# A GNN–LSTM–GNN kernel: one LSTM chain is set four steps behind the other, and two batches of each end's layers go between turns of a single chain

## The chip, the cores and the metric

The kernel runs on one core of a Trainium2 chip. The metric is device microseconds of one execution; less is better. All data is float32. TensorE multiplies in its float32r form; a float32 operand is split into a high part and a remainder, and a product is three matmuls (high × high, high × low, low × high).

## The reference

`x` is [16, 512, 128] (batches, tokens, features), `adj` is [512, 512]. What is computed is:

```
h  = relu(layernorm(x))
h  = relu(adj @ (h @ Wg0 + bg0));  h = relu(adj @ (h @ Wg1 + bg1))      # per batch
for p in 1..4:                      # windows of p tokens, the last token of each is replaced
    wins = h[:, :nw*p].reshape(16*nw, p, 128)                           # nw = 512 // p
    h[:, p-1::p] = last hidden state of an LSTM with weights p over wins  # p steps
x  = x + h
g  = relu(layernorm(x))
A_hat = D^-1/2 (adj + I) D^-1/2
t  = relu(batchnorm((A_hat @ g) @ W1.T + b1))      # 256 features, statistics over all 16*512 rows
x  = x + batchnorm(t @ W2.T + b2)                  # 128 features
```

## The kernel before, in words

It is written engine by engine; each engine runs a fixed list of instructions, and semaphores tie the lists together. The order of the lists is set by tables of numbers at the head of the file.

**LSTM turns.** Features lie on the partitions, tokens along the free axis. The 16 batches go in four rounds of four; a round has two chains, each of two batches (`CHAINS`, `SUBS`). A chain makes 11 turns a round (`STEPS`, L40): two for p=1 (one per batch, 512 windows), then the 2, 3 and 4 steps of p=2, 3, 4 for both batches together (512, 340 and 256 windows). A turn (`lstm_turn`: TensorE L1087, ScalarE L580, VectorE L814) is: gate products into PSUM banks (three gates on the first step of a window, four after), sigmoid/tanh on ScalarE (L598), cell update on VectorE (L836 to L844), tanh of the cell on ScalarE (L608), hidden state on VectorE (L849/L851 between the steps of a window, L870 at its end). On steps after the first the input tokens need their own split: the high part on ScalarE (L606), the low part on GpSimd (`later_class`, L352 to L356). A p=1 turn ends with four VectorE operations: odd tokens into `cell` (L857), their high part (L859) and low part (L669), and the even tokens into `h32` (L864).

**Slots.** `ORDER` (L41) sets the 22 turns of a round in a row: the p=1 turns of chain 0 and 1 first, then step for step the one chain after the other. A turn is a slot; 88 slots in all. The slot loops (TensorE L1114, VectorE L875, ScalarE L611, GpSimd L358) put other batches' work behind the turns, from two tables:

- `PRE_POS` (L99): layer norm of `x` ("stats" on VectorE, then `layer_norm` on GpSimd, L328 to L340, then "norm", the hi/lo split, L550 and L664) and four product units `AGG0`, `LIN0`, `LIN1`, `AGG1` of the first GNN, for the batches of the next round. `EARLY = 4`: those of batches 0 to 3 lie in a prologue (`PROLOGUE`, L264), as does part of batch 4's.
- `POST_POS` (L101): for the batches of the round before, "turn" (transpose back and residual, L1047 and L759), "stats" and "norm" of the second layer norm, "agg" (A_hat product, L1055), "hid0", "hid1" (the two halves of the W1 product, L1062, with a PSUM eviction L573 and statistics L770). Those of the last four batches (12 to 15) lie in a tail (L1143).

In round 0 the slots also hold the degree sums of `adj` (`deg_steps`, L1066) and four chunks of A_hat (`HAT_CHUNK`, L774 to L788 on VectorE). SyncE issues the loads, stores and spills in one list (from L403).

**Final stage.** After the statistics of all batches comes batch norm 1. Scale and shift of its 32 halves of 512 tokens (L389) are on GpSimd (30) and VectorE (2, `DVE_HALVES`); ScalarE takes relu and the high part (L648), VectorE the low part (L667), TensorE the W2 product, ScalarE its eviction (L641), VectorE its statistics (L944). Then come batch norm 2 (L658, L398), transposes and the residual.

Of the kernel before, what the change touches and what calls it, by code (L numbers as in the profile page):

```python
# [21 lines left out]
ALU = mybir.AluOpType  # L22
# [68 lines left out]
DVE_HALVES = (0, 1)  # L91
# [3 lines left out]
EARLY = PER_ROUND  # L95
# [7 lines left out]
IN_PROLOGUE = [(kind, EARLY + b) for kind, spots in PRE_POS.items() for b in range(PER_ROUND) if spots[b] < 0]  # L103
PRE_AFTER = [[(kind, n) for kind, spots in PRE_POS.items() for n in range(EARLY, BATCHES)
              if len(ORDER) * (n // PER_ROUND - 1) + spots[n % PER_ROUND] == slot] for slot in range(N_SLOTS)]
POST_AFTER = [[(kind, n) for kind, spots in POST_POS.items() for n in range(LATE)
               if len(ORDER) * (n // PER_ROUND + 1) + spots[n % PER_ROUND] == slot] for slot in range(N_SLOTS)]


DEG_SUM, DEG_TOKENS, DEG_POW, DINV_DIAG, DINV_ROWS = 3, 3, 4, 5, 7  # L110
HAT_CHUNK = (8, 11, 14, 17)
# [13 lines left out]
def build(nc, x, adj, Wg0, bg0, Wg1, bg1, Wih, Whh, bih, bhh, W1, b1, g1, be1, W2, b2, g2, be2, out):  # L125
# [7 lines left out]
    with whole:  # L133
# [13 lines left out]
        minus_half, minus_one, eps = (sb(n, [P, CHUNKS]) for n in ("minus_half", "minus_one", "eps"))  # L147
# [28 lines left out]
        ln_pre = [sb(f"ln_pre{i}", [P, 3, CHUNKS]) for i in range(2)]  # L176
        ln_post = [sb(f"ln_post{i}", [P, 3, CHUNKS]) for i in range(2)]
# [39 lines left out]
        def f32(ap):  # L217
# [36 lines left out]
        t_dve, t_pool, hid_hi, hid_lo, out_mm, z2_ready, z2_stats = (  # L254
            sem(n) for n in ("t_dve", "t_pool", "hid_hi", "hid_lo", "out_mm", "z2_ready", "z2_stats"))
# [10 lines left out]
        for _pair in range(2):  # L266
            for _k in range(4):
                PROLOGUE += [(_k, 2 * _pair), (_k, 2 * _pair + 1)]
                if _k in (AGG0, LIN1) and _pair == 0:
                    PROLOGUE += [("stats" if _k == AGG0 else "norm", n) for n in (2, 3)]  # L270
                if _k in (AGG0, LIN1) and _pair == 1:
                    PROLOGUE += [(kind, n) for kind, n in IN_PROLOGUE if kind == ("stats" if _k == AGG0 else "norm")]
                if 6 + 4 * _pair + _k < len(BANKS):
                    PROLOGUE.append(("bank", 6 + 4 * _pair + _k))

        def pre_number(n, k):

            return 8 * (n // 2) + 2 * k + n % 2 if n < EARLY else 4 * n + k

# [34 lines left out]
        def _(pool):  # L314
# [6 lines left out]
            for tile, value in ((minus_half, -0.5), (minus_one, -1.0), (eps, EPS)):  # L321
# [6 lines left out]
            def layer_norm(n, y, src, mv, ln, stats, ready):  # L328
# [4 lines left out]
                nc.gpsimd.tensor_tensor(ln[:, 2, :], mv[:, :, 0], minus_one[:, :], ALU.mult)  # L333
# [23 lines left out]

            for slot in range(N_SLOTS):  # L358
                r, chain, p, step, sub, nb = TURNS[slot]
                if p >= 3 and step + 1 < p:  # L360
                    later_class(r, chain, p, step + 1)
# [11 lines left out]
            for n in range(LATE, BATCHES):  # L373
# [10 lines left out]
            for k, b in enumerate(END_ORDER):  # L384
                if b < SPILLED:
                    pool.wait_ge(z_in[b], 16)
                for half in ((1,) if k in DVE_HALVES else (0, 1)):
                    zz = z_end(b)[:, half * T:(half + 1) * T]
                    last = nc.gpsimd.tensor_scalar(zz, zz, bn1[:, 4, half:half + 1], bn1[:, 5, half:half + 1],  # L389
                                                   ALU.mult, ALU.add)  # L390
                last.then_inc(t_pool, 1)
# [11 lines left out]
        def _(sp):  # L403
# [42 lines left out]
            for r in range(ROUNDS):  # L446
                m, n = PER_ROUND * (r + 1), PER_ROUND * (r - 1)
                if r == 0:
                    load_x_pre(m)
                    load_x_pre(m + 1)  # L450
# [51 lines left out]
        def _(act):  # L502
# [77 lines left out]
            def lstm_turn(g):  # L580
# [4 lines left out]
                for j, gt in enumerate(gates_of(step)):  # L585
                    if prev is not None and TURNS[prev][2] == 1:

                        if gt == G_GATE:
                            act.wait_ge(h_done, prev + 1)
                            act.wait_ge(even_done, FIRST_BEFORE[prev + 1])  # L590
# [7 lines left out]
                    nc.scalar.activation(gate[:, tile_of(g), gt, 0:size], gate_ps[k % GATE_BANKS][:, 0:size],  # L598
# [607 lines left out]
```

## Time and profile before

| | |
|---|---|
| time, median of 3 runs | 613.42 us (611.78 to 615.2) |
| the profiled execution: its own time / its span | 614.24 us / 612.4 us |
| TensorE matmul busy | 526.4 us (86%), 2769 matmuls |
| VectorE busy | 434.4 us (71%) |
| ScalarE busy | 349.7 us (57%) |
| GpSimd busy | 208.2 us (34%) |
| mean granted TensorE clock | 0.947 |
| first gate matmul starts | 71.31 us |
| last hidden state written | 518.05 us |
| batch norm 1 starts | 548.71 us |

The span runs from the first to the last instruction. Stages by time: up to 71 us prologue; 71 to 518 us the 88 turns (rounds 0 to 3 of 113, 117, 117 and 99 us from last tanh to last tanh, the first from the stage's start); to 549 us the tail's layers; then the final stage. A busy figure of TensorE includes the drain of each matmul, which overlaps the next.

### The profile page before, as it was taken

The numbers are of one execution on the slowest core, as the hardware profiler recorded it, in microseconds if no ns is written. First come the engines' busy times: TensorE is split into PE (matmuls) and PEld (weight loads), VectorE is DVE, ScalarE is ACT, GpSimd is POOL, SyncE is SP. The second block draws the span as 40 slices with busy tenths as digits, with TensorE's granted clock in tenths as the row PEclk, the third lists the DMA queues.
The fourth block names the chain that finished last, engine by engine and source line by source line (L and its number), as shares of the span: only waits on it lengthen the run. The fifth ranks groups of instructions, "written<-read, shape, count | busy, mean of one in ns | idle before, by whom it ended". The sixth has DMA issues, their size and how long they took to land.

```text
span 612.4 us, 8136 instructions
## 1 busy us (share of the span) xinstructions
PE 526.4 (86%) x2769; PEld 450.7 (74%) x2769; DVE 434.4 (71%) x985; ACT 349.7 (57%) x660; POOL 208.2 (34%) x316
## 2 busy tenths in 40 slices
PE   4579899698999899999989999998699988766646
PEld 3467768597987688988977798997487988545436
DVE  3364476877886888778588887866867876557766
ACT  2523565555556567666665665756647765245654
POOL 2241003311340266247005560600143240809951
PEclk9769999989899999999999999999989989796997
DMA  6200002000001110202011101004510000500007
GB/s 215 78 4 33 2 0 87 18 18 1 18 1 36 51 52 34 71 1 70 25 62 51 36 35 52 18 35 153 226 34 1 18 18 14 194 0 0 0 0 276
DMA packets 17837, 31.21 MB, mean 51 GB/s; under 512 B 1498, under 2 KB 6020, under 8 KB 17796
## 3 DMA queue, kind: packets, MB, share of 16 engines
q1 hardware_dynamic: 17092, 30.30, 14.5%
q8 instruction: 22, 0.36, 0.3%
q10 hardware_dynamic: 704, 0.39, 0.2%
q14 instruction: 19, 0.16, 0.1%
HBM read 19.16 MB, written 11.53 MB: 50 GB/s over the span
## 4 chain that ended last, share of the span: by engine, by line
PE 47%; issue 23%; DVE 11%; POOL 11%; ACT 4%; POOLq 2%; DVEq 0%; ACTq 0%
PE gate_ps L972 10%; PE gate_ps L974 9%; PE gate_ps L973 9%; POOL z_back L389 5%; PE pre_ps L973 3%; PE pre_ps L974 3%; PE pre_ps L972 3%; POOL x_pre L338 3%; PE post_ps L972 2%; PE post_ps L974 2%; PE post_ps L973 2%; POOLq L336 2%; ACT gate L608 1%; POOL z_ring L389 1%; ACT gate L598 1%
## 5 line engine op out<-in xcount | busy, mean ns | idle before, releaser
L598 ACT ACTIVATE gate<-gate_ps,gate_bias 128x256 f32<-128x256 f32 (+2 forms) x312 | 166.6, 565 | 55.6 <-PE gate_ps L974 53.1
L972 PE MATMUL gate_ps<-by_class_hi,wih_hi 128*128 128x256 f32 (+2 forms) x264 | 86.8, 329 | 14.1 <-POOL by_class_lo L356 7.2
L608 ACT ACTIVATE gate<-cell 128x512 f32<-128x512 f32 (+2 forms) x88 | 45.3, 515 | 77.7 <-DVE cell L844 41.8
L974 PE MATMUL gate_ps<-by_class_lo,wih_hi 128*128 128x256 f32 (+2 forms) x264 | 85.2, 323 | 0.0
L973 PE MATMUL gate_ps<-by_class_hi,wih_lo 128*128 128x256 f32 (+2 forms) x264 | 85.1, 322 | 0.0
L972 PEld LDWEIGHTS gate_ps<-by_class_hi,wih_hi 128*128 128x128 f32 x264 | 51.4, 195 | 21.3 <-POOL by_class_lo L356 8.0
L972 PE MATMUL gate_ps<-hstep_hi,whh_hi 128*128 128x256 f32 (+2 forms) x192 | 61.5, 320 | 0.0
L973 PE MATMUL gate_ps<-hstep_hi,whh_lo 128*128 128x256 f32 (+2 forms) x192 | 61.5, 320 | 0.0
L974 PE MATMUL gate_ps<-hstep_lo,whh_hi 128*128 128x256 f32 (+2 forms) x192 | 61.4, 320 | 0.0
L332 POOL TENSOR_TENSOR ln_pre<-mv_pre,eps 128x4 f32<-128x4 f32 x16 | 5.0, 314 | 159.2 <-DVE mv_pre L713 159.2
L356 POOL TENSOR_TENSOR by_class_lo<-h,by_class_hi 128x256 fp32r<-128x256 f32 (+1 forms) x40 | 35.3, 890 | 61.2 <-ACT by_class_hi L606 61.2
L973 PEld LDWEIGHTS gate_ps<-by_class_hi,wih_lo 128*128 128x128 f32 x264 | 51.4, 195 | 3.8
L974 PEld LDWEIGHTS gate_ps<-by_class_lo,wih_hi 128*128 128x128 f32 x264 | 51.2, 194 | 2.3
L332 POOL TENSOR_TENSOR ln_post<-mv_post,eps 128x4 f32<-128x4 f32 x16 | 6.1, 381 | 136.7 <-DVE mv_post L713 136.7
L849 DVE TENSOR_TENSOR gate<-gate 128x256 f32<-128x256 f32 (+2 forms) x48 | 26.9, 560 | 26.4 <-ACT gate L608 26.4
L973 PEld LDWEIGHTS gate_ps<-hstep_hi,whh_lo 128*128 128x128 f32 x192 | 37.8, 197 | 1.3
L974 PEld LDWEIGHTS gate_ps<-hstep_lo,whh_hi 128*128 128x128 f32 x192 | 37.7, 197 | 1.3
L972 PEld LDWEIGHTS gate_ps<-hstep_hi,whh_hi 128*128 128x128 f32 x192 | 37.7, 196 | 1.3
L338 POOL TENSOR_SCALAR x_pre<-x_pre,ln_pre 128x128 f32<-128x128 f32 x64 | 35.7, 569 | 2.8 <-issue 2.8
L338 POOL TENSOR_SCALAR y_post<-x,ln_post 128x128 f32<-128x128 f32 x56 | 34.8, 633 | 2.5 <-issue 2.5
L838 DVE TENSOR_TENSOR gate<-gate 128x256 f32<-128x256 f32 (+2 forms) x48 | 24.3, 507 | 15.8 <-ACT gate L598 15.8
L389 POOL TENSOR_SCALAR z_back<-z_back,bn 128x512 f32<-128x512 f32 x24 | 29.7, 1253 | 0.0
(249 smaller groups left out, 1406.7 us busy)
## 6 DMA issues: line engine op xcount, KB each, us to landing
x_pre<-in_x SPq DMA_DIRECT2D x16, 256.0 KB, 2.6
x<-in_x SPq DMA_DIRECT2D x16, 256.0 KB, 2.8
z_spill<-z_ring SPq DMA_DIRECT2D x8, 512.0 KB, 2.7
z_back<-z_spill SPq DMA_DIRECT2D x8, 512.0 KB, 7.4
x_spill<-x SPq DMA_DIRECT2D x12, 256.0 KB, 2.0
x_back<-x_spill SPq DMA_DIRECT2D x1, 3072.0 KB, 11.1
out<-x_back SPq DMA_DIRECT2D x12, 256.0 KB, 2.2
x<-in_adj SPq DMA_DIRECT2D x1, 1024.0 KB, 5.5
```

The costliest lines, as they stand in the source:

```text
L332: nc.gpsimd.tensor_tensor(ln[:, 0, :], mv[:, :, 1], eps[:, :], ALU.add)
L336: nc.gpsimd.drain()
L338: last = nc.gpsimd.tensor_scalar(y[:, c * P:(c + 1) * P], src[:, c * P:(c + 1) * P], ln[:, 2, c:c + 1], ln[:, 1, c:c + 1], ALU.add, ALU.mult)
L356: nc.gpsimd.tensor_tensor(lo, states, f32(hi), ALU.subtract).then_inc(later_lo, 1)
L389: last = nc.gpsimd.tensor_scalar(zz, zz, bn1[:, 4, half:half + 1], bn1[:, 5, half:half + 1], ALU.mult, ALU.add)
L598: nc.scalar.activation(gate[:, tile_of(g), gt, 0:size], gate_ps[k % GATE_BANKS][:, 0:size], ACT.Tanh if gt == G_GATE else ACT.Sigmoid, bia ...
L608: nc.scalar.activation(gate[:, tile_of(g), G_GATE, 0:size], cell[:, tile_of(g), 0:size], ACT.Tanh)\
L838: nc.vector.tensor_tensor(i_, i_, g_, ALU.mult).then_inc(ig_done, 1)
L849: nc.vector.tensor_tensor(i_, o_, g_, ALU.mult).then_inc(h_done, 1)
L972: nc.tensor.matmul(ps, w[0], m[0], start=start, stop=False)
L973: nc.tensor.matmul(ps, w[1], m[0], start=False, stop=False)
L974: return nc.tensor.matmul(ps, w[0], m[1], start=False, stop=stop)
```

## The change

- **Slots.** A round still has 22 turns, but chain 0 has the even slots and chain 1 the odd ones, and chain 1 runs `LAG = 4` steps behind. There are 97 slots. Slots 1, 3, 5 and 7 have no turn and slots 0, 2, 4, 6 and 8 one of chain 0; slots 89 to 95 have turns of chain 1 alone, 88 to 96 even ones none.
- **Input layers.** `EARLY` goes from 4 to 2: in the prologue stay, of batch 2, "stats", "norm", `AGG0` and `LIN0`; the rest of batch 2 goes to slots 1 and 3, batch 3 to slots 3 to 9.
- **Output layers.** The tail has batches 14 and 15 alone (`TAIL`); those of 12 and 13 lie in slots 88 to 96. All positions of `PRE_POS` and `POST_POS` are new, as are those of the degree sums and A_hat chunks. The list of SyncE follows.
- **Even tokens** of a p=1 turn: off VectorE (L864), onto ScalarE as a copy out of `cell` (L639 of the new file). In the new file VectorE's next first cell update waits for it.
- **Layer norm on GpSimd** loses one of its small operations: the mean is no longer multiplied by −1 (L333), it is subtracted straight from `mv`.
- **Batch norm 1 halves**: GpSimd 30 → 25, VectorE 2 → 1, ScalarE 0 → 6.

```diff
-ORDER = ([(chain, s) for chain in range(CHAINS) for s in range(SUBS)]
-         + [(chain, s) for s in range(SUBS, len(STEPS)) for chain in range(CHAINS)])
-N_SLOTS = ROUNDS * len(ORDER)
+LAG = 4
+ROUND = CHAINS * len(STEPS)
+N_SLOTS = ROUND * ROUNDS + CHAINS * LAG + 1
+def step_in(slot):
+    chain = slot % CHAINS
+    r, s = divmod(slot // CHAINS - LAG * chain, len(STEPS))
+    return (r, chain, s) if 0 <= r < ROUNDS else None
...
-DVE_HALVES = (0, 1)
+DVE_HALVES = ((0, 0),)
+ACT_HALVES = ((0, 1), (3, 1), (5, 1), (8, 1), (11, 1), (14, 1))
...
-EARLY = PER_ROUND
-PRE_POS = {"stats": (-5, 4, 7, 13), "norm": (-2, 6, 10, 16),
-           AGG0: (0, 8, 13, 18), LIN0: (1, 10, 14, 19), LIN1: (2, 11, 15, 20), AGG1: (4, 12, 17, 21)}
-POST_POS = {"turn": (0, 1, 2, 3), "agg": (6, 9, 14, 19), "hid0": (7, 10, 16, 20), "hid1": (8, 11, 17, 21),
-            "norm": (5, 7, 12, 17), "stats": (3, 5, 9, 15)}
+EARLY = SUBS
+TAIL = BATCHES - SUBS
+PRE_POS = {"stats": (6, 11, 15, 25), "norm": (8, 13, 18, 26),
+           AGG0: (10, 16, 20, 27), LIN0: (11, 17, 21, 28), LIN1: (13, 18, 23, 29), AGG1: (15, 19, 25, 31)}
+POST_POS = {"turn": (0, 1, 9, 10), "agg": (3, 6, 13, 16), "hid0": (4, 7, 14, 17), "hid1": (5, 8, 15, 18),
+            "norm": (2, 5, 12, 15), "stats": (0, 2, 9, 12)}
...
-HAT_CHUNK = (8, 11, 14, 17)
+HAT_CHUNK = (10, 13, 16, 19)
...
                 nc.gpsimd.tensor_tensor(ln[:, 0, :], mv[:, :, 1], eps[:, :], ALU.add)
-                nc.gpsimd.tensor_tensor(ln[:, 2, :], mv[:, :, 0], minus_one[:, :], ALU.mult)
...
+            def even_tokens(g):
+                r, chain, p, step, sub, nb = TURNS[g]
+                act.wait_ge(h_done, g + 1)
+                if r > 0:
+                    act.wait_ge(turn_mm, batch_of(r - 1, chain, sub) + 1)
+                nc.scalar.activation(h32[:, chain, 0::2, sub], cell[:, chain, 0:T // 2], ACT.Copy)\
+                    .then_inc(even_done, 1)
...
+            for slot, g in enumerate(TURN_AT):
+                if g is not None:
+                    lstm_turn(g)
                 for splits in (True, False):
+                    if not splits and g is not None and TURNS[g][2] == 1:
+                        even_tokens(g)
...
+            def hid_t(k, half):
...
+                nc.scalar.activation(zz, zz, ACT.Identity, bias=bn1[:, 5, half:half + 1],
+                                     scale=bn1[:, 4, half:half + 1]).then_inc(t_act, 1)
...
+                    if PREV[g] is not None and TURNS[PREV[g]][2] == 1:
+                        before = TURNS[PREV[g]]
+                        dve.wait_ge(even_done, FIRST_BEFORE[PREV[g] + 1])
+                        dve.wait_ge(class_lo, CLASS_AT[before[0], chain, 1, before[4]])
                     dve.wait_ge(gates_act, k + 2)
                     nc.vector.tensor_tensor(c_, i_, g_, ALU.mult).then_inc(cell_ready, 1)
...
-                    if r > 0:
-                        dve.wait_ge(turn_mm, batch_of(r - 1, chain, sub) + 1)
-                    nc.vector.tensor_tensor(h32[:, chain, 0::2, sub], gate[:, tile_of(g), O_GATE, 0:T // 2],
-                                            gate[:, tile_of(g), G_GATE, 0:T // 2], ALU.mult).then_inc(even_done, 1)
```

The first place is GpSimd's list at the end of round 0 and the start of round 1. `by_class_lo` is the low part of an LSTM input (`later_class`), `ln_pre`/`x_pre` a first layer norm, `ln_post`/`y_post` a second one, `mv` mean and variance. Before:

```order
L332 TENSOR_TENSOR ln_pre<-mv_pre,eps 128x4
L333 TENSOR_TENSOR ln_pre<-mv_pre,minus_one 128x4
L335 TENSOR_TENSOR ln_pre<-ln_pre,minus_half 128x4
L338 TENSOR_SCALAR x_pre<-x_pre,ln_pre 128x128 x4
L356 TENSOR_TENSOR by_class_lo<-h,by_class_hi 128x256 x2
L332 TENSOR_TENSOR ln_post<-mv_post,eps 128x4
L333 TENSOR_TENSOR ln_post<-mv_post,minus_one 128x4
L335 TENSOR_TENSOR ln_post<-ln_post,minus_half 128x4
L338 TENSOR_SCALAR y_post<-x,ln_post 128x128 x4
```

and after the change:

```order
L388 TENSOR_TENSOR by_class_lo<-h,by_class_hi 128x340
L365 TENSOR_TENSOR ln_post<-mv_post,eps 128x4
L367 TENSOR_TENSOR ln_post<-ln_post,minus_half 128x4
L370 TENSOR_SCALAR y_post<-x,mv_post,ln_post 128x128 x4
L388 TENSOR_TENSOR by_class_lo<-h,by_class_hi 128x256
L365 TENSOR_TENSOR ln_post<-mv_post,eps 128x4
L367 TENSOR_TENSOR ln_post<-ln_post,minus_half 128x4
L370 TENSOR_SCALAR y_post<-x,mv_post,ln_post 128x128 x4
L388 TENSOR_TENSOR by_class_lo<-h,by_class_hi 128x256
L365 TENSOR_TENSOR ln_pre<-mv_pre,eps 128x4
```

Before, the first second-layer norm came after all of the round's low parts; now chain 1's p=4 low parts (128x256) lie behind the norms of batches 0 and 1.

The second place is ScalarE's list around the split of batch 7's layer norm (`nrm_hi<-x_pre`). Before:

```order
L598 ACTIVATE gate<-gate_ps,gate_bias 128x256 x4
L606 ACTIVATE by_class_hi<-h 128x256
L608 ACTIVATE gate<-cell 128x256
L552 ACTIVATE nrm_hi<-x_pre 128x512
L598 ACTIVATE gate<-gate_ps,gate_bias 128x256 x4
L606 ACTIVATE by_class_hi<-h 128x256
L608 ACTIVATE gate<-cell 128x256
L557 ACTIVATE lstm_in_hi<-pre_ps 128x512
```

and after the change:

```order
L630 ACTIVATE gate<-cell 128x512
L639 ACTIVATE h<-cell 128x256
L575 ACTIVATE nrm_hi<-y_post 128x512
L620 ACTIVATE gate<-gate_ps,gate_bias 128x256 x4
L628 ACTIVATE by_class_hi<-h 128x256
L630 ACTIVATE gate<-cell 128x256
L580 ACTIVATE lstm_in_hi<-pre_ps 128x512
L601 ACTIVATE agg_hi<-post_ps 128x512
L620 ACTIVATE gate<-gate_ps,gate_bias 128x512 x3
L630 ACTIVATE gate<-cell 128x512
L575 ACTIVATE nrm_hi<-x_pre 128x512
L596 ACTIVATE z_ring<-post_ps,vec 128x512
```

The split of batch 7 stood in slot 16, three slots behind its "stats"; it now stands in slot 26, one slot behind them. `h<-cell` is the new even-token copy.

## Rows read from the trace of the kernel before

**Rows 1.** The page: busy time, share, instructions of TensorE.
```profile
PE 526.4 (86%) x2769; PEld 450.7 (74%) x2769; DVE 434.4 (71%) x985; ACT 349.7 (57%) x660; POOL 208.2 (34%) x316
```
**Rows 2.** Busy time by stretch; per engine (instructions), then clock, DMA share, GB/s.
```profile
103.00:190.00 87.00, 78.11 (x455) 71.12 (x454) 67.12 (x150) 48.71 (x105) 23.94 (x36) 0.94 0.05 13
190.00:306.00 116.00, 111.55 (x628) 97.87 (x627) 90.38 (x216) 74.67 (x146) 43.72 (x66) 1.00 0.12 42
423.00:518.00 95.00, 83.83 (x457) 72.63 (x456) 71.33 (x163) 62.42 (x124) 26.91 (x38) 0.95 0.20 69
```
**Rows 3.** Timeline of TensorE in round 1 (start, length, operation).
```profile
276.38 0.28 PE L974 MATMUL gate_ps<-hstep_lo,whh_hi 128*128 128x256 f32 x1
276.50 0.40 PE L972 MATMUL pre_ps<-adj_t_hi,u_hi 128*128 128x512 f32 x1
276.73 0.40 PE L973 MATMUL pre_ps<-adj_t_hi,u_lo 128*128 128x512 f32 x1
```
**Rows 4.** Timeline of GpSimd and of TensorE behind it, round 0.
```profile
117.19 0.37 POOL L332 TENSOR_TENSOR ln_pre<-mv_pre,eps 128x4 f32<-128x4 f32 x1 [11.45 <-DVE mv_pre L713]
121.52 0.90 POOL L356 TENSOR_TENSOR by_class_lo<-h,by_class_hi 128x340 fp32r<-128x340 f32 x1
122.48 0.65 PE L972 MATMUL gate_ps<-by_class_hi,wih_hi 128*128 128x340 f32 x1 [4.88 <-POOL by_class_lo L356]
```
**Rows 5.** The clock behind two waits: windows as in rows 2.
```profile
122.00:132.00 10.00, 9.52 (x44) 9.34 (x45) 6.83 (x13) 5.10 (x11) 2.41 (x3) 0.71 0.01 2
440.00:450.00 10.00, 6.73 (x23) 5.09 (x22) 8.11 (x25) 4.89 (x8) 5.82 (x9) 0.83 0.16 53
```
**Rows 6.** GpSimd's four scalings of a second norm, in round 1 and in the tail.
```profile
211.68 2.35 POOL L338 TENSOR_SCALAR y_post<-x,ln_post 128x128 f32<-128x128 f32 x4 [0.17 <-issue]
522.60 1.73 POOL L338 TENSOR_SCALAR y_post<-x,ln_post 128x128 f32<-128x128 f32 x4 [0.17 <-issue]
```
**Rows 7.** Timeline of VectorE: cell and odd tokens of a p=1 turn.
```profile
199.19 0.68 DVE L844 TENSOR_TENSOR cell<-gate 128x512 f32<-128x512 f32 x1
200.57 0.69 DVE L857 TENSOR_TENSOR cell<-gate 128x512 f32<-128x512 f32 x1 [0.70 <-ACT gate L608]
```
**Rows 8.** Groups by line and shape: busy, mean ns, idle before.
```profile
L864 DVE TENSOR_TENSOR h<-gate 128x256 f32<-128x256 f32 x16 | 9.8, 614 | 0.0
L606 ACT ACTIVATE by_class_hi<-h 128x256 fp32r<-128x256 f32 x24 | 11.0, 459 | 0.0
```
**Rows 9.** TensorE's first gate matmul.
```profile
71.31 0.50 PE L972 MATMUL gate_ps<-lstm_in_hi,wih_hi 128*128 128x512 f32 x1 [1.63 <-DVE w_lo L669]
```
**Rows 10.** An A_hat chunk on VectorE, first and last operation.
```profile
168.26 0.66 DVE L778 TENSOR_TENSOR z_ring<-adj_t_hi,adj_t_lo 128x512 f32<-128x512 f32 x1
170.65 0.82 DVE L669 TENSOR_TENSOR hat_lo<-z_ring,hat_hi 128x512 fp32r<-128x512 f32 x1
```
**Rows 11.** Last hidden state, and batch norm 1.
```profile
517.63 0.42 DVE L870 TENSOR_TENSOR h<-gate 128x256 f32<-128x256 f32 x1 [0.48 <-ACT gate L608]
548.71 1.03 DVE L917 BATCH_NORM_AGGREGATE bn<-stats 128x2 f32<-128x96 f32 x2
```
**Rows 12.** Groups as in rows 8, of the final stage.
```profile
L389 POOL TENSOR_SCALAR z_back<-z_back,bn 128x512 f32<-128x512 f32 x24 | 29.7, 1253 | 0.0
L667 DVE SCALAR_TENSOR_TENSOR hid_lo<-z_back,hid_hi 128x1024 fp32r<-128x1024 f32 x12 | 15.9, 1324 | 7.0 <-ACT hid_hi L648 7.0
L648 ACT ACTIVATE hid_hi<-z_back 128x1024 fp32r<-128x1024 f32 x12 | 12.6, 1052 | 9.3 <-POOL z_back L389 9.3
L641 ACT ACTIVATE z_back<-gate_ps,vec 128x512 f32<-128x512 f32 x12 | 8.1, 676 | 2.2 <-PE gate_ps L974 2.2
L944 DVE BATCH_NORM_STATS2 stats<-z_back 128x6 f32<-128x512 f32 x12 | 8.0, 680 | 0.7 <-ACT z_back L641 0.7
L658 ACT ACTIVATE z_back<-z_back,bn 128x512 f32<-128x512 f32 x8 | 5.7, 800 | 0.0
L398 POOL TENSOR_SCALAR z_back<-z_back,bn 128x512 f32<-128x512 f32 x4 | 3.0, 767 | 0.0
```

More of the change, by code:

```diff
@@ L103 @@
[L103 to L107, printed above, removed]
@@ new lines, with pre_slot, post_slot @@
+POST_POS = {"turn": (0, 1, 9, 10), "agg": (3, 6, 13, 16), "hid0": (4, 7, 14, 17), "hid1": (5, 8, 15, 18),
+            "norm": (2, 5, 12, 15), "stats": (0, 2, 9, 12)}
+def pre_slot(kind, n):
+    return ROUND * (n // PER_ROUND - 1) + PRE_POS[kind][n % PER_ROUND]
+def post_slot(kind, n):
+    return ROUND * (n // PER_ROUND + 1) + POST_POS[kind][n % PER_ROUND]
+IN_PROLOGUE = [(kind, n) for n in range(EARLY, BATCHES) for kind in PRE_POS if pre_slot(kind, n) < 0]
+PRE_AFTER = [[(kind, n) for kind in PRE_POS for n in range(EARLY, BATCHES) if pre_slot(kind, n) == slot]
+             for slot in range(N_SLOTS)]
@@ L112 @@
+POST_AFTER = [[(kind, n) for kind in POST_POS for n in range(TAIL) if post_slot(kind, n) == slot]
+              for slot in range(N_SLOTS)]
+DEG_SUM, DEG_TOKENS, DEG_POW, DINV_DIAG, DINV_ROWS = 2, 2, 3, 5, 7
+HAT_CHUNK = (10, 13, 16, 19)
 SPLITS = (AGG0, LIN0, LIN1, AGG1, "turn", "agg")
@@ L265, in build @@
                                                             ("bank", CHUNKS + 1), ("norm", 0), ("norm", 1)])
[L266 to L274, printed above, removed]
+        for _k in range(4):
+            PROLOGUE += [(_k, 0), (_k, 1)]
+            if _k in (AGG0, LIN1):
+                PROLOGUE += [(kind, n) for kind, n in IN_PROLOGUE if kind == ("stats" if _k == AGG0 else "norm")]
+            PROLOGUE += [("bank", 6 + 2 * _k), ("bank", 7 + 2 * _k)]
+        assert PROLOGUE[-1] == ("bank", len(BANKS) - 1)
+        PROLOGUE += [(kind, n) for kind, n in IN_PROLOGUE if kind in (AGG0, LIN0)]
         def pre_number(n, k):
-            return 8 * (n // 2) + 2 * k + n % 2 if n < EARLY else 4 * n + k
+            return 2 * k + n if n < EARLY else 4 * n + k
         def z_new(n):
@@ L356, in later_class @@
                 nc.gpsimd.tensor_tensor(lo, states, f32(hi), ALU.subtract).then_inc(later_lo, 1)
[L358 to L361, printed above, removed]
+            for slot, g in enumerate(TURN_AT):
+                if g is not None:
+                    r, chain, p, step, sub, nb = TURNS[g]
+                    if p >= 3 and step + 1 < p:
+                        later_class(r, chain, p, step + 1)
                 for kind, n in PRE_AFTER[slot]:
@@ L386, in _ @@
                     pool.wait_ge(z_in[b], 16)
[L387 to L391, printed above, removed]
+                for half in range(HALVES):
+                    if (k, half) in POOL_HALVES:
+                        zz = z_end(b)[:, half * T:(half + 1) * T]
+                        nc.gpsimd.tensor_scalar(zz, zz, bn1[:, 4, half:half + 1], bn1[:, 5, half:half + 1],
+                                                ALU.mult, ALU.add).then_inc(t_pool, 1)
             pool.wait_ge(bn2_var, 1)
@@ L818, in lstm_turn @@
                 size = nb * windows
-                i_, f_, g_, o_ = (gate[:, tile_of(g), gt, 0:size] for gt in range(4))
-                c_ = cell[:, tile_of(g), 0:size]
+                i_, f_, g_, o_ = (gate[:, chain, gt, 0:size] for gt in range(4))
+                c_ = cell[:, chain, 0:size]
                 k = GATES_BEFORE[g]
@@ L873, in lstm_turn @@
                         first_class(p + 1)
-            for slot in range(N_SLOTS):
-                lstm_turn(slot)
+            for slot, g in enumerate(TURN_AT):
+                if g is not None:
+                    lstm_turn(g)
                 for splits in (True, False):
@@ L1112, in lstm_turn @@
                     last.then_inc(gates_mm, 1)
-            for slot in range(N_SLOTS):
-                lstm_turn(slot)
+            for slot, g in enumerate(TURN_AT):
+                if g is not None:
+                    lstm_turn(g)
                 deg_steps(slot)
```

173 lines of the change are left out of this document (85 added, 88 removed).

## The prediction, made before the changed kernel was run

> **What bounds the kernel now.** I read the page's engine line first: TensorE is busy 86% of the span, VectorE 71% [rows 1]. The reader should see two candidates, and that TensorE leads. Then the busy time by stretch: round 1 is nearly full, 111.6 of 116 us, at clock 1.00; round 0 has 78.1 of 87 and round 3 83.8 of 95 [rows 2]. So TensorE sets the pace where other batches' work lies between the turns, and waits where that work is missing (round 3) or comes late (round 0).
>
> Next the timeline gives TensorE's pace, start to start: a 128x256 matmul 0.12 us, a 128x512 one 0.23 us [rows 3]; for 128x128 I take 0.11. With the counts of the program, 3 matmuls to a product, a chain needs 30.2 us of TensorE a round; the input layers of a batch (12, 12, 4 and 1 matmuls of 512, 12 of 128) 8.0 us; its output layers (18 of 512, 4 of 128) 4.6 us; degree sums and A_hat 7.5 us. A full round needs 2 × 30.2 + 4 × 8.0 + 4 × 4.6 = 110.8 us, beside the 111.6 busy that row 2 shows. By the same sum round 0 needs 99.9 and round 3 78.8. Against 113, 117, 117 and 99 us of length, TensorE waits 13, 6, 6 and 20 us in the four rounds: some 46 us of the 447 between the first gate matmul at 71.3 [rows 9] and the last hidden state at 518.05 [rows 11]. These waits and the two ends are what the change can win.
>
> How such a wait looks: GpSimd started a layer norm at 117.19, the low part that chain 0's turn needed stood behind it until 121.52, and TensorE waited 4.88 us [rows 4]. The granted clock of the ten microseconds after is 0.71; after a wait of 3.3 us at 444 it is 0.83 [rows 5]. That is a mixture of the two levels, 1.2 and 2.4 GHz.
>
> **The change, part by part.**
>
> *Start.* 12.3 us of TensorE's work (8.0 of batch 3, LIN1 and AGG1 of batch 2, 4.3) leave the prologue, and about 1.7 us of waits between them: −14. The first gate comes at about 57. This work isn't saved, it is +12.3 in round 0.
>
> *End.* 9.2 us of work of batches 12 and 13 leave the tail, now 30.7 us long [rows 11]. I walked the rest by durations of before: 18 us remain, −12.5. The work is +9.2 between slots 88 and 96.
>
> *Round 0.* Slots 0 to 8 have chain 0 alone. "stats" of batch 3 are made after turn 3, its norm on GpSimd takes 4.4 us (117.2 to 121.5 [rows 4]), the split is two operations of 512 columns, some 0.7 each, and AGG0 of batch 3 is the only filler of its slot: a wait of 5.7 us, then 2.6 at the lower clock. LIN1 of batch 3 waits about 2 behind its eviction. In slots 13 to 18 VectorE has A_hat chunks of 3.2 us (168.26 to 171.47 [rows 10]) beside batch 4's and 5's evictions: six waits of 0.7 to 2.2, 10 in sum. Together 20.8 against 13: **+8**.
>
> *Round borders 0/1, 1/2, 2/3.* Before, the second norms came after the round's last low parts. Now the first stands ahead of the low part of chain 1's second p=4 step (the first place shown). The norm's four scalings alone are 2.35 us beside a busy VectorE, 1.73 in the tail [rows 6]; with its statistics and small operations ahead of it TensorE waits 3.9 us in slot 25. In slot 26 ScalarE's list holds batch 7's split one slot behind its statistics (the second place), so AGG0 comes about 3.1 us late, and all of ScalarE's list behind it, `hid0`'s eviction first. "turn" of the odd batch waits 1.5 us for its buffer, slots 34 to 36 about 3.3. Sum 11.8 against 6; with the norm at 1.73 it is 9.4. I take 10 against 6, which over two such rounds and the border before round 3 makes **+8** in rounds 1 and 2 (bounds +7 and +12).
>
> *Round 3 to slot 96.* Slots 78 to 82: 3.8 us for GpSimd's norm of batch 10, 1.9, 2.0. In slots 89 to 95 chain 1 runs p=4 alone; a turn's path through the engines is longer than its matmuls, and "agg" of 12 and 13 fill two gaps of about four: 14 us. With the rest 29.9 against 20.6; I take **+8** (bounds +4 and +10).
>
> *Even tokens.* Sixteen VectorE operations of 0.61 us go; 16 ScalarE copies come, whose nearest row is 0.46 us [rows 8]. In a p=1 turn VectorE is the longer engine: from cell at 199.19 it waits 0.70 us for the tanh and has three operations behind [rows 7]. So up to 0.6 us a turn where VectorE sets the pace, nothing where TensorE does; it is within the waits above. The new wait at the next first cell update holds up what follows on VectorE only if ScalarE is late; between the two lies a whole turn of four to seven gates. I price it at 0, bounds 0 and +3.
>
> *Layer norm.* One small GpSimd operation of 0.2 to 0.3 us less for each of 32 norms, up to −2 where a norm decides. Zero; the cover is GpSimd's idle time.
>
> *Final stage.* Now GpSimd's halves, 24 at 1.25 us and some more, set it: 30 halves, 36.6 us. The same kind of operation is 0.77 us where VectorE has no two-input work [rows 12]. After: GpSimd 25 × 1.24 = 31; ScalarE 16 × 1.05 + 16 × 0.68 + 6 × 0.80 = 32.5; VectorE 16 × 1.32 + 16 × 0.68 + 0.7 = 32.8, all from [rows 12]. Bound by the last, −4 (bounds −2, if the three get in each other's way, and −6). The row says that GpSimd slows when VectorE works beside it, by 1.25 against 0.77. The Trainium skill, GPSIMD Engine Reference, section "Specifications" (Terminology), gives a reason: the two share their SBUF interfaces, with contention when VectorE reads two SBUF inputs. By it GpSimd would slow further as VectorE's share rises: estimated 1.34 × 25 = 33.5, a gain of 3.1 instead of 4.
>
> *Sum.* −14 + 12.3 + 9.2 + 8 + 8 + 8 − 12.5 − 4 = +15. The profiled execution's own time is 614.2, 0.8 above the median; 613.4 + 15 = **628 us**. Of it the pure move is −5 (21.5 us of work inserted, 26.5 taken from the ends), and the waits are +24.
>
> **The rivals.**
>
> *A, faster.* The waits don't grow. My walk takes each queue's order as strict and every norm at its slow price; queues run ahead where TensorE is behind. For A: the staggering puts one chain's p=1 turns, VectorE's longest, beside the other chain's p=3 steps instead of four in a row, and round 1 shows that full slots reach 96% [rows 2]. Against: the same row shows how little is left to win there. Waits as before give 613.4 − 14 − 12.5 + 21.5 − 4 = **604**; 15 us fewer give 589. It decides if the waits in sum grow by less than about 6.
>
> *B, nothing.* The waits grow by 9, a third of what I walked: **613**.
>
> *C, far slower.* Each new wait of 3 to 4 us brings back the lower clock. A stretch of 10 us after one had 0.83 [rows 5]: 1.7 us of it at full worth, six to eight such waits, +12: **640**. For it speaks the 0.71 of the same rows; against it, that work stands ready behind most of these waits. The Trainium skill, TensorE: Matmul & The Clock Gate, part "The HAM clock gate", says that an array which sits idle falls to 1.2 GHz and has to work before it gets 2.4 back; the trace agrees with the 0.71 behind 4.88 us. It speaks against this change, which puts lone chains at both ends, and only C counts it in full.
>
> *The forecast turned by one mechanism* would be A: the place is slots 25, 47, 69, the price 3.9 us each, and it decides by whether `later_class` of chain 1 gets ahead of the norm.
>
> **How the numbers follow.** Forecast 0.47, with its own range 618 to 638 (waits +14 to +34); A 0.33; B 0.10; C 0.10. Over 0.5%, 3 us, is about what a measurement can tell: faster 0.33, same 0.10, slower 0.57. The range is 597 to 641: A's lower part (waits 7 us fewer and beyond) and C's upper part are left out, about 0.1 each.
>
> **What would show it.** First gate matmul near 57 us, last hidden state near 549, batch norm 1 near 567, final stage near 60 us. Round 1's busy share below the 96% of before; in the waits, TensorE for GpSimd's low part in slots 25, 47 and 69, 3 to 4 us each; a clock under 0.9 in slots 3 to 8 and 89 to 96. Wrong, if the last hidden state comes before 533: then the waits didn't grow, and A holds. If the final stage is still over 63 us, the halves weren't the bound.

## The result: 673.4 us, slower by 9.75%

The changed kernel takes 673.43 us (median of 6 runs, 670.84 to 678.42) against 614.7 of the kernel before: a ratio of 1.0975, 95% interval 1.094 to 1.101. The forecast was slower, and 628; the range ended at 641. Nearly 60 us were lost where 15 were forecast. The profiled execution is the slowest of the six, 678.4. The kernel before was timed again beside each group of experiments, with medians of 614.5 (e), 613.1 (f), 613.6 (g) and 613.5 (h), so a difference between two groups is uncertain by about a microsecond. One of the four executions of f4 took 1306.7 us, twice the others, and is left out.

The page of the changed kernel, its first rows (busy time, share, instructions of each engine):

```profile
span 676.6 us, 8143 instructions
...
PE 548.5 (81%) x2769; PEld 470.6 (70%) x2769; DVE 431.2 (64%) x968; ACT 366.0 (54%) x682; POOL 237.9 (35%) x278
```

TensorE's share fell from 86 to 81% [rows 1]. GpSimd has 38 instructions fewer than before and is busy 30 us longer. The groups by line and shape (busy, mean ns, idle time before) name the place:

```profile
L370 POOL TENSOR_SCALAR x_pre<-x_pre,mv_pre,ln_pre 128x128 f32<-128x128 f32 x64 | 58.4, 924 | 2.8 <-issue 2.8
L370 POOL TENSOR_SCALAR y_post<-x,mv_post,ln_post 128x128 f32<-128x128 f32 x60 | 56.2, 948 | 2.6 <-issue 2.6
```

Before the change the same scalings were:

```profile
L338 POOL TENSOR_SCALAR x_pre<-x_pre,ln_pre 128x128 f32<-128x128 f32 x64 | 35.7, 569 | 2.8 <-issue 2.8
L338 POOL TENSOR_SCALAR y_post<-x,ln_post 128x128 f32<-128x128 f32 x56 | 34.8, 633 | 2.5 <-issue 2.5
```

A norm has four of them, so they take 1.3 to 1.4 us more, less 0.2 to 0.3 for the small operation that went. What TensorE waited for in the changed kernel, in us altogether, times, longest:

```profile
PE gate_ps L1017 <- POOL by_class_lo L388: 30.8, 8, 5.6
PE pre_ps L1017 <- DVE nrm_lo L714: 26.5, 5, 7.5
PE gate_ps L1017 <- DVE hid_lo L714: 13.5, 5, 8.0
PE gate_ps L1017 <- DVE nrm_lo L714: 8.2, 1, 8.2
```

Before, the wait for GpSimd's low parts was this:

```profile
PE gate_ps L972 <- POOL by_class_lo L356: 7.2, 3, 4.9
```

The timeline at the border of rounds 0 and 1 shows one of the eight, with the norm of batch 0 and then the low part on GpSimd, and TensorE behind it:

```profile
183.94 0.29 POOL L365 TENSOR_TENSOR ln_post<-mv_post,eps 128x4 f32<-128x4 f32 x1 [18.62 <-DVE mv_post L760]
184.37 1.07 POOL L367 TENSOR_TENSOR ln_post<-ln_post,minus_half 128x4 f32<-128x4 f32 x1
185.62 4.09 POOL L370 TENSOR_SCALAR y_post<-x,mv_post,ln_post 128x128 f32<-128x128 f32 x4 [0.18 <-issue]
189.67 1.19 POOL L388 TENSOR_TENSOR by_class_lo<-h,by_class_hi 128x256 fp32r<-128x256 f32 x1
190.92 0.58 PE L1017 MATMUL gate_ps<-by_class_hi,wih_hi 128*128 128x256 f32 x1 [5.56 <-POOL by_class_lo L388]
```

The four scalings take 4.09 us where the same place of the round had 2.35 before [rows 6]. Twenty us on, ScalarE stands before batch 7's split, with `hid0`'s eviction and four gates queued behind it, and TensorE's AGG0 waits:

```profile
209.80 0.63 ACT L575 ACTIVATE nrm_hi<-x_pre 128x512 fp32r<-128x512 f32 x1 [4.21 <-POOL x_pre L370]
210.34 0.67 ACT L596 ACTIVATE z_ring<-post_ps,vec 128x512 f32<-128x512 f32 x1
210.91 1.56 ACT L620 ACTIVATE gate<-gate_ps,gate_bias 128x256 f32<-128x256 f32 x4
211.30 0.77 PE L1017 MATMUL pre_ps<-adj_t_hi,nrm_hi 128*128 128x512 f32 x1 [3.94 <-DVE nrm_lo L714]
211.87 0.63 PE L1018 MATMUL pre_ps<-adj_t_hi,nrm_lo 128*128 128x512 f32 x1
212.29 0.63 PE L1019 MATMUL pre_ps<-adj_t_lo,nrm_hi 128*128 128x512 f32 x1
```

Behind this wait the matmuls of 512 columns start 0.42 to 0.43 us apart, where they started 0.23 apart in rows 3; the granted clock from 212 to 216 us is 0.50, the lower of the two levels. Both waits come again at each border. Busy time by stretch (columns as in rows 2): chain 0 alone, most of round 1, and chain 1 alone at the end:

```profile
62.00:102.00 40.00, 30.47 (x122) 24.27 (x121) 19.61 (x49) 14.60 (x24) 10.18 (x13) 0.81 0.10 33
190.00:306.00 116.00, 108.06 (x580) 95.52 (x581) 78.39 (x185) 68.22 (x132) 44.69 (x52) 0.94 0.12 42
560.00:592.00 32.00, 22.58 (x108) 19.21 (x106) 13.67 (x34) 11.53 (x25) 11.28 (x14) 0.77 0.00 1
```

In the stretch in which round 1 had 628 matmuls at clock 1.00 [rows 2] there are now 580 at 0.94. TensorE looks nearly as busy, 108 us against 112, because its matmuls at the lower level last longer: the count and the clock tell it, not the busy time.

The milestones, first gate matmul, last hidden state (its last write starts), batch norm 1, end of span:

```profile
57.20 0.40 PE L1017 MATMUL gate_ps<-lstm_in_hi,wih_hi 128*128 128x512 f32 x1
592.75 0.43 DVE L917 TENSOR_TENSOR h<-gate 128x256 f32<-128x256 f32 x1 [0.48 <-ACT gate L630]
616.60 1.03 DVE L962 BATCH_NORM_AGGREGATE bn<-stats 128x2 f32<-128x96 f32 x2
```

Before they stood at 71.3, 517.6 and 548.7 of 612.4 [rows 9, 11]. So in the profiled executions the start won 14.1, the stretch of the turns lost 89, the tail won 7, the final stage won 3.7.

### The profile page after: what moved, and what is told of

It reads as the page before. It is cut to its first block, busy times and chain, and to the rows that moved or that the text cites. A ratio compares the mean times of both kernels' runs of the same rounds, so it can differ in the third digit from the quotient of the medians.

```text
span 676.6 us, 8143 instructions
## 1 busy us (share of the span) xinstructions
PE 548.5 (81%) x2769; PEld 470.6 (70%) x2769; DVE 431.2 (64%) x968; ACT 366.0 (54%) x682; POOL 237.9 (35%) x278
## 4 chain that ended last, share of the span: by engine, by line
PE 34%; issue 28%; POOL 15%; DVE 14%; ACT 5%; POOLq 4%; DVEq 1%; ACTq 0%
PE gate_ps L1017 6%; PE gate_ps L1018 6%; PE gate_ps L1019 6%; POOL y_post L370 5%; POOL z_back L423 3%; POOL x_pre L370 3%; PE pre_ps L1017 3%; PE pre_ps L1018 3%; PE pre_ps L1019 3%; POOLq L368 3%; POOL by_class_lo L388 2%; PE post_ps L1017 2%; PE post_ps L1018 2%; ACT gate L630 2%; PE post_ps L1019 2%
## 5 line engine op out<-in xcount | busy, mean ns | idle before, releaser
L1017 PE MATMUL gate_ps<-by_class_hi,wih_hi 128*128 128x256 f32 (+2 forms) x264 | 90.3, 342 | 37.7 <-POOL by_class_lo L388 30.8
L1019 PE MATMUL gate_ps<-by_class_lo,wih_hi 128*128 128x256 f32 (+2 forms) x264 | 87.9, 333 | 0.0
L1018 PE MATMUL gate_ps<-by_class_hi,wih_lo 128*128 128x256 f32 (+2 forms) x264 | 87.8, 333 | 0.0
L1017 PEld LDWEIGHTS gate_ps<-by_class_hi,wih_hi 128*128 128x128 f32 x264 | 54.0, 205 | 45.9 <-POOL by_class_lo L388 34.2
L630 ACT ACTIVATE gate<-cell 128x256 f32<-128x256 f32 (+2 forms) x88 | 45.3, 515 | 51.6 <-DVE cell L895 30.6
L370 POOL TENSOR_SCALAR x_pre<-x_pre,mv_pre,ln_pre 128x128 f32<-128x128 f32 x64 | 58.4, 924 | 2.8 <-issue 2.8
L370 POOL TENSOR_SCALAR y_post<-x,mv_post,ln_post 128x128 f32<-128x128 f32 x60 | 56.2, 948 | 2.6 <-issue 2.6
L1018 PEld LDWEIGHTS gate_ps<-by_class_hi,wih_lo 128*128 128x128 f32 x264 | 54.0, 205 | 3.7
L1017 PE MATMUL pre_ps<-adj_t_hi,nrm_hi 128*128 128x512 f32 x60 | 28.5, 476 | 27.0 <-DVE nrm_lo L714 26.5
L885 DVE TENSOR_TENSOR gate<-gate 128x256 f32<-128x256 f32 (+2 forms) x48 | 24.4, 508 | 39.0 <-ACT gate L620 38.8
L900 DVE TENSOR_TENSOR gate<-gate 128x256 f32<-128x256 f32 (+2 forms) x48 | 30.2, 629 | 29.0 <-ACT gate L630 29.0
```

The source lines that it names most:

```text
L630: nc.scalar.activation(gate[:, chain, G_GATE, 0:size], cell[:, chain, 0:size], ACT.Tanh)\
L885: nc.vector.tensor_tensor(i_, i_, g_, ALU.mult).then_inc(ig_done, 1)
L900: nc.vector.tensor_tensor(i_, o_, g_, ALU.mult).then_inc(h_done, 1)
L1017: nc.tensor.matmul(ps, w[0], m[0], start=start, stop=False)
L1018: nc.tensor.matmul(ps, w[1], m[0], start=False, stop=False)
L1019: return nc.tensor.matmul(ps, w[0], m[1], start=False, stop=stop)
```

## The experiments

### The norm on GpSimd: a subtract, or an operand

**e1** puts the old form back into the changed kernel:

```diff
+                nc.gpsimd.tensor_tensor(ln[:, 2, :], mv[:, :, 0], minus_one[:, :], ALU.mult)
...
-                                                   mv[:, c, 0:1], ln[:, 1, c:c + 1], ALU.subtract, ALU.mult)
+                                                   ln[:, 2, c:c + 1], ln[:, 1, c:c + 1], ALU.add, ALU.mult)
```

> The changed kernel with layer norm on GpSimd as before the change: mean times -1, then add and multiply from the same small tile. In the changed kernel's profile the scaling takes 924 and 948 ns where it was 569 and 633 ns before, so a norm is some 1.4 us longer, less 0.3 for the operation that went. Theory N (the form of the norm is the main cause of the lost 59 us): the scalings go back to 0.57-0.65 us and over 30 us come back, 673 -> 643 or less. Theory O (the new order is the cause; the form only adds about 1.1 us to each of the some 14 waits of TensorE that end on a norm or on a low part behind one): some 15 us come back, 656 to 661. Theory F (nothing but contention with VectorE: the form plays no part): the scalings stay over 0.9 us and the time within 5 us of 673.

Measured: 653.2 us (ratio to before 1.064, 1.059 to 1.070), 20 us back; between theories N and O, nearer O's 15. The scalings are short again, and the waits at the first border are 3.38 us for the low part and 3.00 for batch 7's split:

```profile
L371 POOL TENSOR_SCALAR x_pre<-x_pre,ln_pre 128x128 f32<-128x128 f32 x64 | 35.0, 559 | 2.8 <-issue 2.8
183.53 0.58 PE L1018 MATMUL gate_ps<-by_class_hi,wih_hi 128*128 128x256 f32 x1 [3.38 <-POOL by_class_lo L389]
202.08 0.47 PE L1018 MATMUL pre_ps<-adj_t_hi,nrm_hi 128*128 128x512 f32 x1 [3.00 <-DVE nrm_lo L715]
```

**e2** is the opposite, the new form alone in the kernel before.

> The kernel before with the new form of the layer norm alone. Theory N: the scalings go to 0.9 us, and the time rises by over 15 us, to 630 or more. Theory O: the scalings go to 0.9 us too, but in the old order few norms decide a wait (one of 4.9 us in round 0), so +2 to +8, 616 to 622. Theory F: scalings stay at 0.57-0.63 us, time 611 to 615.

Measured: 624.8 us (1.017, 1.013 to 1.021): +10.2, above O's range and below N's. **e3** and **e4** separate the two things that the edit changed; e4's result is not the norm's, as it adds the mean where it should subtract it.

> The kernel before with its small operation kept as a copy (times +1) and subtract in the scaling, so the operand's place is the old one and only the operation is new; same result. If the operation (subtract) costs the 0.35 us: L338 at about 0.9 us. If the operand's place (the mean read straight from mean and variance) costs it: L338 stays at 0.57-0.63 us and the time at 611 to 616.

> The kernel before without the small operation, the scaling with add as before but reading the mean straight from mean and variance (so it adds the mean where it should subtract it). If the operation costs: the scaling stays at 0.57-0.63 us. If the operand's place costs: about 0.9 us.

The scaling of the first norm in e3 (subtract, old operand) and in e4 (add, new operand), by line and shape:

```profile
L338 POOL TENSOR_SCALAR x_pre<-x_pre,ln_pre 128x128 f32<-128x128 f32 x64 | 58.9, 930 | 2.8 <-issue 2.8
```
```profile
L337 POOL TENSOR_SCALAR x_pre<-x_pre,mv_pre,ln_pre 128x128 f32<-128x128 f32 x64 | 36.5, 582 | 2.8 <-issue 2.8
```

It is the operation: GpSimd's `tensor_scalar` with subtract takes 930 ns where the one with add takes 582. The operand's place costs nothing that shows: with add, the first norm's scalings go from 569 to 582 ns with the new operand and the second's from 633 to 629. Nor is it something that VectorE does beside it. In the tail, where the same scalings are at their shortest in both kernels, the difference is as large (e3, then e4):

```profile
L338 POOL TENSOR_SCALAR cell<-x,ln_post 128x128 f32<-128x128 f32 x8 | 6.3, 798 | 0.3 <-issue 0.3
L337 POOL TENSOR_SCALAR cell<-x,mv_post,ln_post 128x128 f32<-128x128 f32 x8 | 3.6, 460 | 0.3 <-issue 0.3
```

The times agree, with one execution of each: 627.1 for e3, 614.1 for e4.

### The order at the borders

All of these start from e1's kernel. **f2** issues each second norm one slot later, behind that slot's low part:

```diff
+            held = []
...
-                for kind, n in POST_AFTER[slot]:
-                    if kind == "stats":
-                        norm_post(n, y_post)
+                for n in held:
+                    norm_post(n, y_post)
+                held = [n for kind, n in POST_AFTER[slot] if kind == "stats"]
```

> The changed kernel with the old form of the norm (653.2 us), and with every second norm on GpSimd one slot later, behind that slot's low part. Theory O (the place of the norm ahead of chain 1's low parts costs five waits of 3.4 to 3.9 us and the clock behind them): these waits go, -15 to -25, 628 to 638. Theory R (the waits only move to the next link, since the norm itself is then late for its split and its A_hat product): under 7 us come back, 646 or more.

Measured: 637.7 us (1.039, 1.036 to 1.042), 15.5 back. The waits for GpSimd's low parts at the borders are gone from the timeline; the wait for batch 7's split rose only from 3.0 to 3.33. Theory O.

**g1** then moves what hangs on the fourth batch of each round by one slot:

```diff
-PRE_POS = {"stats": (6, 11, 15, 25), "norm": (8, 13, 18, 26),
-           AGG0: (10, 16, 20, 27), LIN0: (11, 17, 21, 28), LIN1: (13, 18, 23, 29), AGG1: (15, 19, 25, 31)}
+PRE_POS = {"stats": (6, 11, 15, 25), "norm": (8, 13, 18, 27),
+           AGG0: (10, 16, 20, 28), LIN0: (11, 17, 21, 29), LIN1: (13, 18, 23, 30), AGG1: (15, 19, 25, 31)}
```

> The kernel of f2 (637.7 us) with the split of the first norm of each round's last batch (7, 11, 15) and its first three product units one slot later. TensorE waits 3.3 us three times for that split there. Theory O (each border wait is a matter of one slot in a queue): two or three of 3.3 go, -5 to -10. Theory R (it moves to the next link: the units now follow each other in neighbouring slots): within 3 us of 637.7.

Measured: 616.9 us (1.005, 1.003 to 1.007), 20.8 back, twice what theory O allowed. The three waits of 3.33 us are gone, and the 6.54 before batch 3's product is now one of 3.93 before a gate product: 12.6 us of waits. Added up, all of TensorE's waits in the stretch of the turns fell by 14.0 us (51.1 to 37.1), and the stretch by 21.3 (499.1 to 477.8). The rest is time in which TensorE worked and was slower; the next experiment tests that by itself. The same stretch in f2 and in g1:

```profile
190.00:306.00 116.00, 108.01 (x602) 95.05 (x601) 84.10 (x195) 72.16 (x140) 40.17 (x65) 0.97 0.12 44
```
```profile
190.00:306.00 116.00, 111.21 (x621) 97.30 (x621) 88.23 (x210) 75.97 (x150) 39.45 (x64) 1.00 0.14 46
```

**g2** leaves the order of f2 and fills four waits with idle matmuls:

```diff
                 if k == AGG0:
+                    if n >= SUBS and n % PER_ROUND == PER_ROUND - 1:
+                        for _ in range(22 if n == PER_ROUND - 1 else 12):
+                            nc.tensor.matmul(ps[:, :], adj_t[0][:, 0, 0:P], adj_t[0][:, 0, :], start=True, stop=True)
                     pe.wait_ge(pre_nlo, n + 1)
```

> The kernel of f2 (637.7 us) with idle work: 22 matmuls of 512 ahead of the first product of batch 3 and 12 ahead of those of batches 7, 11 and 15, into the PSUM bank that the product overwrites; 5 and 2.8 us of TensorE's time, inside waits of 6.5 and 3.3 us. Theory K (the lower clock behind a wait is a large part of its price): the granted clock of the span rises from 0.928, and 4 to 10 us come back. Theory W (the wait alone is the price): within 2 us of 637.7, or +1 to +3 where the filling overruns.

Measured: 631.3 us (1.029, 1.026 to 1.031), 6.4 us less for 58 matmuls more. The stretch around slot 27 in f2 and in g2:

```profile
196.00:216.00 20.00, 17.77 (x77) 14.94 (x78) 12.09 (x27) 10.89 (x21) 5.32 (x10) 0.83 0.15 53
```
```profile
196.00:216.00 20.00, 20.00 (x109) 17.42 (x110) 14.54 (x33) 13.21 (x27) 6.85 (x12) 1.00 0.16 53
```

In f2 the granted clock of the 20 us is 0.83, a mixture of 1.2 and 2.4 GHz behind a wait of 3.33 us; with the wait filled it is 1.00. It did 32 matmuls more, 12 of them idle. So the clock behind a wait is a price of its own: 6.4 us over four waits of 16.5 us in sum. Theory K. The Trainium skill, TensorE: Matmul & The Clock Gate, part "The HAM clock gate", has the rule that an idle array falls to 1.2 GHz; the trace agrees, 0.83 against 1.00.

### The other parts

**f1**, the new share of batch norm 1's halves alone in the kernel before:

> The kernel before with the new share of batch norm 1's halves alone (GpSimd 25, VectorE 1, ScalarE 6). Theory S (the sum of the prediction): the final stage goes from 63.7 to 59-60 us, -3 to -4, time 610.5 to 611.5. Theory C (the three engines get in each other's way): less than 2 us, the halves on GpSimd go from 1.25 to over 1.4 us.

Measured: 610.2 us (0.994, 0.992 to 0.996), −3. The halves on GpSimd:

```profile
L400 POOL TENSOR_SCALAR z_back<-z_back,bn 128x512 f32<-128x512 f32 x20 | 26.9, 1359 | 0.0
```

They rose from 1253 ns [rows 12] to 1359. By the trace all halves on GpSimd together take 32.9 us where they took 36.6, and the final stage 60.1 where it took 63.7; by the medians of the whole kernel it is 3.0. GpSimd has no idle time among its halves and VectorE is busy 76% of that time, so GpSimd still sets the stage, and not VectorE as the sum had it; the sum's 32.8 us came out at 32.9 by luck.

The mean hides two kinds. Before, twelve of the 24 halves in rows 12 take 0.76 to 0.77 us and twelve 1.73 to 1.75; in f1 eight take 0.77 and again twelve 1.73 to 1.83. The slow ones lie for 63 to 72% of their time beside VectorE's `hid_lo` (L667 before, two inputs from SBUF), of which there are twelve in rows 12; the fast ones for at most 63%, most of them under 50%. ScalarE isn't it: halves that it works beside from end to end take 0.77 us. So twelve slow halves now weigh on 20 in place of 24, and that is why the mean rose. The Trainium skill, GPSIMD Engine Reference, section "Specifications", says that GpSimd and VectorE contend for their shared SBUF interfaces when VectorE reads two SBUF inputs; the trace agrees, 1.73 us against 0.77. The prediction's estimate by it, 1.34 us for each of 25 halves, was near the 1.32 measured.

**f3** puts the even tokens back on VectorE in e1's kernel (the edit of the change, undone).

> The changed kernel with the old form of the norm (653.2 us) and the even tokens back on VectorE. The ScalarE copy measured 0.68 us, above the 0.61 on VectorE. If the copy on ScalarE costs (it stands ahead of the gates of the next turn, 16 times): -3 to -8. If the old place costs more (VectorE is the longer engine of a p=1 turn): +2 to +8. The prediction had 0 to 3 for it: then 650 to 653.

Measured: 656.5 us (1.070, 1.067 to 1.072), +3.3. That is little more than the scatter: the four executions of e1 lie between 651.5 and 655.2, those of f3 between 654.2 and 656.8. The new place gives about 3, though its copy takes 0.68 us and not 0.46; h2 below is the second case.

**f4** (output layers of 12 and 13 back in the tail) and **g3** (input layers of 2 and 3 back in the prologue, on f2's kernel) undo the two moves.

```diff
-EARLY = SUBS
+EARLY = PER_ROUND
...
-              for n in range(TAIL) if post_slot(kind, n) == slot]
+              for n in range(LATE) if post_slot(kind, n) == slot]
```

(The first pair of lines is g3's, which has the prologue of before with it, the second f4's, with the tail of before.)

> The changed kernel with the old form of the norm (653.2 us), the output layers of batches 12 and 13 back in the tail; slots 88 to 96 keep chain 1's four turns alone. By the prediction the move gives 12.5 us at the tail and costs 9.2 of work, less what lies in waits that are there anyway: the lone turns wait 16 us even with fillers. Theory G (the fillers lie in gaps that a lone chain leaves): +5 to +12, 658 to 665. Theory Z (they give nothing): 650 to 656.

> The kernel of f2 (637.7 us) with all input layers of batches 2 and 3 back in the prologue (EARLY = 4), so slots 1 to 9 have only chain 0's turns and the degree sums. By the prediction the move gave -14 at the start and cost 12.3 of work and 8 of waits, +6: undone, 630 to 633. If the fillers lie in gaps that chain 0 alone leaves anyway, undoing costs: 641 to 650.

Measured: 652.9 (against 653.2) and 638.2 us (against 637.7). Neither move is worth anything measurable. In f4 the last hidden state's write starts at 560.95 and batch norm 1 at 591.67; in e1 at 569.79 and 591.37: the work only changes sides. Theory Z for f4; for g3 neither theory, as the layers come at no net cost.

### Do the parts add up, and can both kernels be beaten

**h1** is the changed kernel with only the two moves of order, f2's and g1's, its norm as it is.

> The changed kernel as it is, with subtract in its norm, and only the two moves of order: each second norm behind the next slot's low part, and batches 3, 7, 11 and 15 one slot later. The two moves gave 36.3 us where the norm had its old form (653.2 -> 616.9). Theory P (the parts add up; a norm 1.1 us longer is paid 14 times anyway): 673 - 36 = 637, 633 to 641. Theory I (the longer norm is only paid where the order leaves it no slack; with a slot of slack it is hidden): 617 to 625, so over 10 us less than the sum.

Measured: 628.6 us (1.024, 1.022 to 1.027), between the two theories, slightly nearer I. Without slack the subtract costs 20.2 us (673.4 − 653.2), with a slot of slack 11.7 (628.6 − 616.9). The norms are as slow as ever:

```profile
L370 POOL TENSOR_SCALAR x_pre<-x_pre,mv_pre,ln_pre 128x128 f32<-128x128 f32 x64 | 61.3, 967 | 2.8 <-issue 2.8
```

**g4** takes to the kernel before what had given time: f1's halves, the even tokens on ScalarE, and every norm on GpSimd, first and second, behind the next slot's low part. **h2** is g4 without the last.

> The kernel before with three parts: batch norm 1's halves shared as in the change (610.2 us alone), the even tokens on ScalarE, and each norm on GpSimd one slot later, behind that slot's low part. Theory O (low parts first removes waits there too: 4.9 us in round 0, 3.3 us in round 3) with the even tokens' -3: 600 to 606. Theory R (the old order was tuned and waits only move): 608 to 614.

> The kernel of g4 (599.8 us) without its third part: batch norm 1's halves and the even tokens as in the change, the norms on GpSimd in their old place. If the even tokens on ScalarE give the -3 here that they gave in the changed kernel: 606 to 608, and the low parts first gave 6 to 8 of g4's 14. If the even tokens alone explain g4 (VectorE is the longer engine of the four p=1 turns that stand in a row in the old order): 600 to 603.

Measured: g4 599.8 us (0.976, 0.973 to 0.978), h2 605.3 (0.987, 0.985 to 0.989). So the halves give 3, the even tokens 4.9 (610.2 → 605.3), the low parts first 5.4 (605.3 → 599.8), by medians of three groups. g4 beats both kernels. The wait of 4.88 us for a low part in round 0 [rows 4] is one of 1.49 there:

```profile
122.59 0.39 PE L1004 MATMUL gate_ps<-by_class_hi,wih_hi 128*128 128x340 f32 x1 [1.49 <-issue]
```

## Why the prediction was wrong in its size

Its direction held, and not by luck: without the subtract, which it had not priced, the changed kernel is still slower (653.2). Its two ends held: the first gate came at 57.2 (forecast 57), the final stage took 60.0 us (60), though GpSimd set it and not VectorE (f1). The failed steps lie between. Of the 45 us between the forecast, 628, and 673.4, the norm is 20.2, the stretch of the turns 20, the tail 3.6, and 1.3 is the median of the kernel before (614.7 against 613.4).

1. **"Layer norm. One small GpSimd operation … less … Zero."** This step priced what the edit removed and not what it swapped: add became subtract in 128 scalings, 0.3 to 0.4 us each. It was never bounded from both sides. Cost: 20.2 us in the changed kernel (e1), 10.2 in the kernel before (e2).

2. **Border waits, right in place.** The walk said 3.9 us in slots 25, 47 and 69 and 3.1 for batch 7's split. With the old norm they are 3.38 and 3.00 (e1); with the subtract 5.56 and 3.94. Batch 3's product in round 0 was to wait 5.7 us and waits 6.55 (e1), 7.50 with the subtract. So the strict reading of each engine's list, which rival A doubted, was right: A is refuted. The last hidden state came at 593, and at 570 with the old norm, far from the 533 that A needed. The other signs came too: round 1's stretch is busy 93%, and the clock is 0.81 and 0.77 where one chain is alone.

3. **The waits of the turns: +24 in the sum, of which 2.6 for the clock.** With the old norm (e1) the stretch of the turns is 512 us where the forecast had 492. Against the 446.3 of before that is 65.9 more, of which the sum counted 21.5 as inserted work. All of TensorE's waits there, added up, are 31.3 us before and 62.8 in e1: 31.5 more. The last 13 are neither work nor wait. In the same stretch the granted clock fell from 0.977 to 0.943; as a mixture of 1.2 and 2.4 GHz that is 20.5 us at the lower level before and 58.0 in e1, and an estimate from the 0.43 and 0.23 us between matmuls gives up to 17 us lost by the 37.5 more. So of the missing 20 about half are waits that the walk didn't find, and about half the clock, which only rival C, with 0.10, counted. g2 and g1 show that price by experiment: filling four waits gave 6.4 us, and moving a batch by one slot gave 20.8 where the waits were 12.6. One reading helped to hide it: the "46 us" that TensorE was said to wait before are what is left beside the work; its waits are 31.3, and the lower clock was already in the rest. (The stretch 440:450 in rows 5 holds the wait itself; from its end at 444.2 on, ten microseconds show the same 0.83.)

4. **Tail, 18 forecast, 23.9 measured** (21.6 in e1). Batches 14's and 15's norms have nothing beside them on TensorE, which waits 8.2 us (6.9 in e1). The walk had it too short.

5. **The moves of layers, −26.5 + 21.5 = −5 in the sum** before waits, are worth 0 to 1 each with the waits they bring (f4, g3).

6. **Even tokens, priced 0 (bounds 0 and +3 of cost):** a gain of 3 (f3, near the scatter) to 5 (h2). Below nothing wasn't allowed in the range, though the same paragraph named the 0.6 us a turn that VectorE saves.

From the changed kernel the account runs 673.4 − 20.2 (norm) − 15.5 (low parts) − 20.8 (fourth batch) = 616.9, by e1, f2 and g1; the shares depend on the order in which they are taken, as h1 shows. What remains against the 605.3 of h2, 11.6 us, is the lag of four steps with its positions and the moved layers. No experiment takes it apart, but the two traces say where it lies: g1's start and tail are 24.3 us shorter than h2's and its stretch of the turns 38.4 longer, with 21.5 of inserted work, 8.6 more of waits, and the clock in that stretch at 0.975 against 0.988.

## What to carry to other kernels

An edit that takes an operation away and changes another has two prices: look for a row of the *new* form before calling it free. In a list that an engine works off in order, ask of each long entry what stands behind it and which slot needs it; a norm one slot too early or a split one slot too early, once a round, cost 15 and 21 us here. The waits of three microseconds and more on TensorE cost more than their length here (6.4 us on top of 16.5 in f2), and a timeline of busy shares hides it, so count matmuls and read the clock. A mean duration can hide two kinds: look at the single operations, and at what runs beside each.

## What was not expected of the hardware

- GpSimd's `tensor_scalar` on 128x128 float32 with subtract and multiply: 924 to 1043 ns in the mean between the turns and 798 in the tail (changed kernel, e2, e3); with add and multiply: 549 to 633 ns and 448 to 464 (before, e1, e4, f2).
- GpSimd's `tensor_scalar` on 128x512 float32 with multiply and add: 0.77 us, or 1.73 where VectorE's `hid_lo` with its two inputs lies beside it for most of that time, and nothing between among the 24 of rows 12 and the 20 of f1.
- ScalarE's copy with a stride on its output, 128x256, 677 ns (changed kernel), where one that writes its operand in a row took 459 [rows 8]. What makes the difference wasn't tried.
